# Norms by slots, idle products and a moved score in a four-layer graph kernel: layer 1's first two norms and layer 2's first on ScalarE and VectorE

## The reference

```python
def _layernorm(x, axis=-1, eps=1e-05):
    m = jnp.mean(x, axis=axis, keepdims=True)
    v = jnp.var(x, axis=axis, keepdims=True)
    return (x - m) / jnp.sqrt(v + eps)
...
        agg = jnp.einsum('nm,bmd->bnd', A_hat, features)          # layer 0
        h = jax.nn.relu(_batchnorm(x @ W1.T + b1, g1, be1))
        out = _batchnorm(h @ W2.T + b2, g2, be2)
...
        e = jnp.einsum('behd,hd->beh', jax.nn.leaky_relu(Xq[:, src] + Xq[:, dst], 0.2), a)   # layer 1
        # + log adj of the edge, softmax over the edges of one src, then
        Y = jax.ops.segment_sum(attn[..., None] * Xv[:, dst], src, num_segments=n)
        return Y @ W_out.T
...
    h = jax.nn.relu(_slconv(x, adj, S, W1))                       # layer 2: (adj*adj) @ (x @ W)
    h = jax.nn.relu(_slconv(h, adj, S, W2))
    return _slconv(h, adj, S, W3)
...
    attention = jax.nn.softmax(where(adj==0, -inf, leaky(s1+s2))) # layer 3
    h_prime = jnp.einsum('bij,bjo->bio', attention, Wh)
```

## Time and profile before

| what | value |
|---|---|
| three runs | 584.73, 585.36 (median), 586.92 us |
| the profiled execution | 586.41 us, its span 584.6 us |
| TensorE busy | 537.5 us (92% of the span) |
| VectorE busy | 423.2 us (72%) |
| ScalarE busy | 370.3 us (63%) |
| GpSimd busy | 210.5 us (36%) |
| mean granted clock of TensorE | 0.96 |

### The profile page before, as it was taken

The page is one execution under the profiler, slowest core; times in us unless marked ns, Lnnn a source line. Parts: engine busy times, 40 slices in busy tenths (PEclk is TensorE's granted clock), DMA queues, the critical chain, the costliest instruction groups (busy, mean ns, idle before and its releaser), DMA issues.

```text
span 584.6 us, 11192 instructions
## 1 busy us (share of the span) xinstructions
PE 537.5 (92%) x3482; PEld 468.7 (80%) x3482; DVE 423.2 (72%) x1454; ACT 370.3 (63%) x741; POOL 210.5 (36%) x248
## 2 busy tenths in 40 slices
PE   3999799589999879999999999999999999999872
PEld 3888433468887679898998998998998998989762
DVE  4688667778986165358879679679778776787887
ACT  3666692557755414536568768778678677675682
POOL 8830530457575240501813513514514314310103
PEclk9999799689999769999999999999999999999997
DMA  7223000221200000000000100100100100100012
...
DMA packets 28383, 15.26 MB, mean 26 GB/s; under 512 B 2320, under 2 KB 28048, under 8 KB 28352
## 3 DMA queue, kind: packets, MB, share of 16 engines
...
...
## 4 chain that ended last, share of the span: by engine, by line
PE 79%; DVE 12%; ACT 4%; issue 2%; POOL 2%; DMA 0%; DVEq 0%; POOLq 0%; ACTq 0%; SPq 0%
PE psum L238 15%; PE psum L240 14%; PE psum L239 14%; PE psum L1818 9%; PE psum L1643 6%; PE psum L1685 5%; PE psum L1760 2%; PE psum L1770 2%; PE psum L1692 2%; PE psum L1696 2%; PE psum L1706 2%; DVE ln_st L184 2%; PE psum L1864 2%; PE psum L1846 2%; POOL ln_r L203 1%
## 5 line engine op out<-in xcount | busy, mean ns | idle before, releaser
L203 POOL TENSOR_TENSOR ln_r<-ln_v,mhalf 128x8 f32<-128x8 f32 x30 | 50.0, 1666 | 238.9 <-DVE ln_v L197 238.9
L1818 PE MATMUL psum<-l2w_s,h 128*128 128x128 f32 x512 | 59.8, 275 | 0.0
L1818 PEld LDWEIGHTS psum<-l2w_s,h 128*128 128x128 f32 x512 | 59.0, 192 | 0.8
L238 PE MATMUL psum<-qt_hi,l2w_s_hi 128*128 128x512 f32 x128 | 52.7, 412 | 0.0
L240 PE MATMUL psum<-qt_hi,l2w_s_lo 128*128 128x512 f32 x128 | 50.7, 396 | 0.0
L239 PE MATMUL psum<-qt_lo,l2w_s_hi 128*128 128x512 f32 x128 | 50.6, 395 | 0.0
L232 ACT ACTIVATE keep_x<-keep_x,ln_b,ln_r (+1 forms) x108 | 44.4, 487 | 7.0 <-DVE keep_x L224 4.4
L1400 ACT ACTIVATE h<-psum 128x512 f32<-128x512 f32 x60 | 34.8, 593 | 11.7 <-PE psum L240 11.6
L184 DVE BATCH_NORM_STATS2 ln_st<-keep_x 128x6 f32<-128x128 f32 (+1 forms) x192 | 39.4, 278 | 2.9 <-ACT keep_x L1328 1.6
L238 PE MATMUL psum<-wgt_hi,h_hi 128*128 128x256 f32 x128 | 37.1, 290 | 0.9 <-DVE h_lo L888 0.9
L240 PE MATMUL psum<-wgt_hi,h_lo 128*128 128x256 f32 x128 | 35.8, 280 | 0.0
...
## 6 DMA issues: line engine op xcount, KB each, us to landing
...
```

Of the source, the lines that this page charges most:

```text
L203: pool.tensor_tensor(ln.r[:].rearrange("p s k -> p (s k)"), ln.v[:].rearrange("p s k -> p (s k)"), mhalf[:], ALU.pow).then_inc(ln.root, 1)
L238: pe.matmul(o, lhs[0], rhs[0], start=start, stop=False)
L1818: i = pe.matmul(bank(s)[:, 0, k * D:(k + 1) * D], h2[:, s, g, j * N + t * P:j * N + (t + 1) * P], l2w3_s[:, g, :], start=(g == 0), stop=(g ...
```

## The change

Six things change, with new semaphores to match.

1. TensorE gets idle products, `spin(n, bank)`: n fp32 products of `ident` with `iota_row` (256 columns) whose result nobody reads. Four stand before the transposes of `dinv` and four behind them, six behind the edge sort, three behind the products for `adj_dst`, and three ahead of the first gather.
2. The layer norms after layer 0 of slots 0 to 3 (`ln0`) and after layer 1 of slots 0 and 1 (`ln1`) are taken slot by slot (`first_stats`, `first_moments`, `first_power`). For slots 0 and 1 VectorE norms two of the four quarters and ScalarE the other two (`first_apply`, `first_scale`); slots 2 and 3 are normed by VectorE alone. ScalarE makes the high half, VectorE the low half, for slots 0 and 1 of `ln0` by graph (`x1_high_low`). GpSimd keeps the powers alone.
3. GpSimd forms `prod` only when VectorE's coefficients (`bn2_ready`) are done.
4. The order ahead of layer 1's loop is `gather(0)`, `project(0)`, `gather(1)`, `score(0)`, `project(1)` among `turn_out` 1 to 4, and the loop begins at 2. ScalarE's `bn_out` runs three steps ahead, no longer four, and slot by slot between the copies of the gathered rows.
5. At the end of layer 1 the order of gather, attend, output and score changes, `turn_attention(0)` moves ahead of `project(6)`, and the second half of step 1's attention goes to bank 2 (before: bank 7).
6. The scores of layer 1's last step are formed inside `mix_x` of layer 2's first step, and VectorE takes the scores (`take_scores(1)`) behind `pt_low`.

```diff
+        def first_stats(dve, q, ln):
+            dve.wait_ge(ln.added, q + 1)
+            for k in range(4):
+                i = dve.bn_stats(ln.st[:, q % 2, k, :], xn[:, q, k // 2, k % 2, :])
+            i.then_inc(ln.one_stats if q < 2 else ln.stats, 1)
+        def first_moments(dve, q, ln, shared):
+            s = q % 2
+            if q < 2:
+                dve.wait_ge(ln.one_stats, q + 1)
+            else:
+                dve.wait_ge(ln.stats, q - 1)
+            for k in range(4):
+                i = dve.bn_aggr(ln.ag[:, s, k, :], ln.st[:, s, k, :])
+            i.then_inc(ln.one_mean, 1)
+            dve.wait_ge(ln.one_mean, q + 1)
+            if shared:
+                dve.tensor_scalar(ln.m[:, s], ln.ag[:, s, :, 0], -1.0, None, ALU.mult)
+            dve.tensor_scalar(ln.v[:, s], ln.ag[:, s, :, 1], LN_EPS, None, ALU.add).then_inc(ln.one_var, 1)
+        def first_power(pool, q, ln, shared):
+            s = q % 2
+            pool.wait_ge(ln.one_var, q + 1)
+            pool.tensor_tensor(ln.r[:, s], ln.v[:, s], mhalf[:, 0:4], ALU.pow).then_inc(ln.one_root, 1)
+            if shared:
+                pool.wait_ge(ln.one_root, q + 1)
+                pool.tensor_tensor(ln.b[:, s], ln.m[:, s], ln.r[:, s], ALU.mult).then_inc(ln.one_rstd, 1)
+        def first_apply(dve, q, ln, ks, done, by):
+            s = q % 2
+            dve.wait_ge(ln.one_root, q + 1)
+            for k in ks:
+                y = xn[:, q, k // 2, k % 2, :]
+                i = dve.tensor_scalar(y, y, ln.ag[:, s, k, 0:1], ln.r[:, s, k:k + 1], ALU.subtract, ALU.mult)
+            i.then_inc(done, by)
+        def first_scale(act, q, ln, ks, done):
+            s = q % 2
+            act.wait_ge(ln.one_rstd, q + 1)
+            for k in ks:
+                y = xn[:, q, k // 2, k % 2, :]
+                i = act.activation(y, y, ACT.Identity, bias=ln.b[:, s, k:k + 1], scale=ln.r[:, s, k:k + 1])
...
             pool.wait_ge(adj_dst_out, 1)
+            pool.wait_ge(bn2_ready, 1)
             pool.tensor_tensor(prod[:], adj_dst[:], ssrc[:], ALU.mult).then_inc(picked, 1)
...
-            ln_power(pool, 0, ln0)
-            for s in range(2):
-                split_x1(0, s, True)
-            ln_power(pool, 1, ln0)
-            with pool.Fori(1, IT - 1) as p:
+            for q in range(4):
+                if q >= 2:
+                    pool.wait_ge(ln0_done[1], q - 1)
+                first_power(pool, q, ln0, q < 2)
+            ln_power(pool, 2, ln0)
+            with pool.Fori(2, IT - 1) as p:
...
-            ln_power(pool, 0, ln1)
-            for s in range(2):
-                split_x(0, s, True)
+            for s in range(2):
+                first_power(pool, s, ln1, True)
+            pool.wait_ge(xs_lo, 2)
...
+            sum0_slot(0, 0)
+            first_stats(dve, 0, ln0)
+            first_moments(dve, 0, ln0, True)
+            sum0_slot(0, 1)
+            first_stats(dve, 1, ln0)
+            first_apply(dve, 0, ln0, (0, 2), ln0_done[0], 1)
+            first_moments(dve, 1, ln0, True)
+            for j in range(2):
+                x1_high_low(0, j)
+            sum0_slot(1, 0)
+            first_apply(dve, 1, ln0, (0, 2), ln0_done[0], 1)
+            first_stats(dve, 2, ln0)
+            for j in range(2):
+                x1_high_low(1, j)
+            first_moments(dve, 2, ln0, False)
+            sum0_slot(1, 1)
+            first_stats(dve, 3, ln0)
+            first_apply(dve, 2, ln0, range(4), ln0_done[0], 2)
+            first_moments(dve, 3, ln0, False)
+            x1_low(2)
+            leaky_slot(0, 0)
+            first_apply(dve, 3, ln0, range(4), ln0_done[1], 2)
+            sum0_slot(2, 0)
+            x1_low(3)
+            sum0_slot(2, 1)
+            leaky_slot(0, 1)
+            variance0(2, False)
+            sum0(3)
+            apply0(2)
+            body(1, False)
+            with dve.Fori(2, IT - 3) as p:
...
+            for s in range(2):
+                leaky_slot(IT - 2, s)
+                weighted_low(0, s)
...
+            weighted_low(1, 0)
+            add(0, 0, o1_done, 1, ln1)
+            first_stats(dve, 0, ln1)
+            first_moments(dve, 0, ln1, True)
+            weighted_low(1, 1)
+            add(0, 1, o1_done, 6, ln1)
+            first_apply(dve, 0, ln1, (0, 2), ln1.done, 1)
+            first_stats(dve, 1, ln1)
+            first_moments(dve, 1, ln1, True)
+            xs_low(0)
+            leaky_slot(IT - 1, 0)
+            first_apply(dve, 1, ln1, (0, 2), ln1.done, 1)
+            xs_low(1)
+            leaky_slot(IT - 1, 1)
...
+                if early:
+                    early(1)
...
+            for p in range(2):
+                for s in range(2):
+                    bn_out_slot(p, s, p == 0)
+            bn_out_slot(2, 0, False)
+            first_scale(act, 0, ln0, (1, 3), ln0_done[1])
+            for j in range(2):
+                x1_high(0, j)
+            bn_out_slot(2, 1, False)
+            first_scale(act, 1, ln0, (1, 3), ln0_done[1])
+            for j in range(2):
+                x1_high(1, j)
+            gathered(0)
+            x1_high_both(2)
+            projected(0, 0)
+            x1_high_both(3)
+            projected(0, 1)
+            for s in range(2):
+                bn_out_slot(3, s, False)
+                gathered_slot(1, s)
+            scale0(2)
+            for s in range(2):
+                projected(1, s)
+            for s in range(2):
+                bn_out_slot(4, s, False)
+            edge_log()
+            scale0(3)
+            with act.Fori(2, IT - 3) as p:
...
+            for s in range(2):
+                gathered_slot(IT - 1, s)
+                y1_turned(0, s, 6 - 6 * s)
+                weighted_high(1, s, False)
+            first_scale(act, 0, ln1, (1, 3), ln1.one_scaled)
+            xs_high(0)
             for s in range(2):
                 projected(IT - 1, s)
...
+                        y1_turned(p + 1, s, 2 if s and first else 6 + s)
...
+            def spin(n, psum_bank):
+                for _ in range(n):
+                    pe.matmul(bank(psum_bank)[:, 0, 0:N], ident[:], iota_row[:], start=True, stop=True)
+            spin(4, 7)
...
             i.then_inc(dinv_spread, 1)
+            spin(4, 7)
...
+            spin(6, 0)
...
             i.then_inc(adj_dst_done, 1)
+            spin(3, 2)
...
             turn_out(0, True)
-            turn_out(1, False)
+            turn_out_slot(1, 0, False)
             pe.wait_ge(picked, 1)
             for t in range(T):
                 i = pe.matmul(bank(6)[:, 0, 0:E], ones[:], prod[:, t, :], start=(t == 0), stop=(t == T - 1))
             i.then_inc(a_edge_done, 1)
+            turn_out_slot(1, 1, False)
+            spin(3, 2)
+            gather(0, True)
             turn_out(2, False)
-            gather(0, True)
+            project(0)
+            gather(1, False)
             turn_out(3, False)
-            project(0)
+            score(0)
+            project(1)
+            turn_out(4, False)
...
+                    if first:
+                        score_slot(IT - 1, s)
...
+                    if first and s == 1:
+                        pe.wait_ge(y1_out, 4)
                     if ahead and not first:
+                        if behind and not two_behind:
+                            pe.wait_ge(sm, SM_STEPS + 1)
...
+            gather_slot(IT - 1, 0, False)
             pe.wait_ge(sm, SM_STEPS)
             attend1(0, 0, 6)
+            gather_slot(IT - 1, 1, False)
+            pe.wait_ge(ln0.added, Q)
+            output1(0, 0, 1)
+            attend1(0, 1, 0)
             score(IT - 2)
-            pe.wait_ge(ln0.added, Q)
-            attend1(0, 1, 0)
+            output1(0, 1, 6)
             project(IT - 1)
-            output1(0, 0, 1)
-            output1(0, 1, 6)
-            score(IT - 1)
             pe.wait_ge(ln1.added, 2)
             attend1(1, 0, 6)
-            pe.wait_ge(sm, SM_STEPS + 1)
-            attend1(1, 1, 7)
+            pe.wait_ge(z_ready, Q - 1)
+            attend1(1, 1, 2)```

TensorE at the first norms of layer 1. Before, from the transposes of `bnt` for slot 2 on (`picked` is GpSimd's `prod`, `x1_lo` a split slot):

```order
L1672 MATMUL psum<-ident,bnt 128x128 [waits ln0_added,bnt_ready]
L1672 MATMUL psum<-ident,bnt 128x128 x3
L1716 MATMUL psum<-prod,ones 128x256 [waits picked]
L1716 MATMUL psum<-prod,ones 128x256
L1672 MATMUL psum<-ident,bnt 128x128 [waits ln0_added,bnt_ready]
L1672 MATMUL psum<-ident,bnt 128x128 x3
L1672 MATMUL psum<-ident,bnt 128x128 [waits ln0_added,bnt_ready]
L1672 MATMUL psum<-ident,bnt 128x128 x3
L1685 MATMUL psum<-sel,x1s_hi 128x512 [waits x1_lo]
```

230 lines of the change are left out of this document (123 added, 107 removed).

## The result

| kernel | runs | median us | lowest to highest | ratio to before, 95% interval |
|---|---|---|---|---|
| before | 4 | 585.97 | 584.73 to 586.92 | 1 |
| changed | 4 | 568.58 | 567.21 to 569.82 | 0.9707 (0.9678 to 0.9736) |

A forecast was written before the change was run, and what follows sets the result against it. TensorE bounds nearly everywhere, save three half-clock stretches, with norm paths holding two layer starts. Terms 1.4 + 2.9 + 3.8 + 12.0 = 20.1 us off 586.41 give 566.3, or 565.3 against the median; range 561.5 to 572.

The forecast's parts named there:

- The end of layer 1: Gather 7 to layer 2's first hidden layers: 24.1 us instead of 36.1, gaining 12.0 us; bounds 7 and 13.9.
- the 13.9 us of loss before: Gather 7 to layer 2's first hidden layers: 36.1 us beyond 22.2 of full-clock work, put down to half clock and waits.
- The second pass: Layer 0's second pass: six idle products keep the clock up, 5.8 us at half clock take 2.9; gain 2.9 us.
- `prod`: Behind the coefficients: GpSimd's `prod`, held until `bn2_ready`, no longer meets VectorE's one-element instruction; gain 0.95 us.
- The start: First products at full clock through idle products, ranking about 1 us sooner; gain 1.4 us, bounds 0 and 2.3.
- The first norms: Layer 1's start up to gather(3): norms slot by slot bring gathers sooner; gain 3.8 us including 0.95 for `prod`.
- the rival with a chance of 0.20: Clock still falls at one or two thin places (`bnt` wait, first norms, layer 2's first step): 569 to 572 us; 0.20.
- the main case: Whole kernel, "as summed": all four terms come out near their forecasts, 562 to 568 us; chance 0.55.
- the case of one or two falls: Whole kernel: TensorE's clock still falls at one or two thin places, 3.4 us each; 569 to 572 us, chance 0.20.
- VectorE beside GpSimd's power: First norms: VectorE's low halves running beside GpSimd's powers lose nothing, going by the earlier trace's row.
- the 1 us that I derived from the rule: First norms: by the skill's shared-pair rule they would lose about 1 us more, four powers deep; not counted.

The follow-up runs named there:

- prod_free: Changed kernel, but GpSimd's `prod` no longer waits for VectorE's coefficients (`bn2_ready`), as before the change; 569.17 us in one run.
- scores_before: Changed kernel with layer 1's last scores, and the leaky steps and copies feeding them, ahead of layer 2's first step; 570.65 us, ratio 0.9747 to before.
- norms_together: Changed kernel with VectorE norming both slots of layer 2's first norm together, ScalarE's and TensorE's orders kept; 573.86 us, ratio 0.9791 to before.

## Why the prediction was right, and where it was off

**The end of layer 1** (12.0 forecast, 12.1 measured) was right in size, and the new state was as walked. TensorE is busy 22.35 us and idle 1.60 us of the 23.95, where the sum had 22.2 and 1.9: 1.02 of `h_hi` and 0.50 of `y1t` make the wait, and taking it away gave 1.9. Counted from gather 7, the split slots are ready after 12.5 and 16.0 us (walked: 12.9 and 15.9) and needed after 14.4 and 16.8 (14.6 and 16.9).

What was wrong is how the 13.9 us of loss before were split. I counted 10.2 us of half clock there; the trace has 17.1 (6.8 from 196.3 on, which the window of 210 to 225 does not see, and 10.2 from 210.0), and TensorE was idle only 6.0 of the 36.06 us. So 7.7 of the 12.1 us are busy time that got shorter (30.06 to 22.35), and 4.4 are waits that went. That did not touch the forecast, which adds up the work that stays.

Undoing parts lost 4.2 (the norm by slots) and 2.1 us (the scores' place), each with a fall of 3.4 us in it. The remaining part, the order of attends, outputs and projection, was not undone alone.

**The second pass** (2.9, measured 2.7) and **`prod`** (0.95, measured 0.94) were each undone alone and lost 2.6 and 0.9 us.

**The start** is the term that was mis-sized: 1.4 forecast, -1.1 measured. The step that failed was "the ranking needs GpSimd's comparisons, which end at 15.9 whatever TensorE does. So it can start about 1 us sooner". The comparisons do set it, but they were 1.44 us late, and then a fall of 3.4 us at 20.1, behind TensorE's wait of 2.36, cost 1.0 (68.8 where 15.48 + 52.3 gives 67.8). With the comparisons at 14.04 and the hop of 52.3 the pass would start 67.73 - (14.04 + 52.3) = 1.4 us sooner, an estimate: the step fails because the comparisons did not stay where they were, and the rest of the term stands. Whether the idle products delay the load stays open: the comparisons began at 14.0, 14.4 and 15.2 in the three kernels without them and at 14.6 to 15.6 in the eleven with them.

**The first norms** were forecast at 2.85 behind `bnt` and gave 2.0. The first gather came 7.1 us behind `bnt` (7.4 walked). Beyond it the clock fell at 139.5, the rival with a chance of 0.20. What that fall costs can be read without an edit: g0-g3 is 36.0 or 36.1 us in the six kernels of the table that have one fall of 3.4 us at 137 to 142 us, and 34.4 in prod_free and scores_before, whose instructions there are the same and whose clock stays up. That is 1.7 us, half of 3.4. Without the fall the term would have been 3.7, above the forecast. The rival's mechanism held beside the main case, at one place and at its price. The total is nearer than its terms: the path without the fall was 0.9 us shorter than summed, and that hid half of what the fall cost.

So 2.5 of the 3.4 us that are missing lie in the start and 0.9 here. The median, 568.58, lies between the main case (562 to 568) and the case of one or two falls (569 to 572). The profiled execution was one of the two upper ones (569.67 and 569.82 against 567.48 and 567.21).

**VectorE beside GpSimd's power.** I priced this at nothing by the earlier trace rows, and that was wrong. Here are the powers of layer 1's first two slots and of layer 2's first one, with VectorE's subtractions of two SBUF inputs that start just ahead of them:

```profile
105.29 1.02 POOL L239 TENSOR_TENSOR ln_r<-ln_v,mhalf 128x4 f32<-128x4 f32 x1 [2.67 <-DVE ln_v L233]
107.85 1.28 POOL L239 TENSOR_TENSOR ln_r<-ln_v,mhalf 128x4 f32<-128x4 f32 x1 [1.26 <-DVE ln_v L233]
191.23 1.38 POOL L239 TENSOR_TENSOR ln_r<-ln_v,mhalf 128x4 f32<-128x4 f32 x1 [4.25 <-DVE ln_v L233]
...
107.84 0.76 DVE L912 TENSOR_TENSOR x1s_lo<-keep_x,x1s_hi 128x256 fp32r<-128x256 f32 x2
191.06 0.68 DVE L971 TENSOR_TENSOR wv_lo<-wv,wv_hi 128x512 fp32r<-128x512 f32 x1
```

A power alone takes 1.01 to 1.03 us. The one that starts 0.01 us after a short subtraction takes 1.27 to 1.29 in all thirteen traces of the changed kernel and its variants. The two of layer 2's first norm start 0.17 us into a long one and take 1.38, except in norms_together, where no subtraction runs beside them and both take 1.01. So a power that starts second pays 0.27 or 0.37 us. VectorE pays nothing: the pair at 107.84 takes 0.76, as at 110.66 with no power beside it, though its second subtraction starts inside the power, and in the earlier trace rows, where the power starts first, neither side pays.

The Trainium skill's rule of the shared pair (SBUF — State Buffer, section "SBUF: two separate sides") says that whoever starts first has it for a whole instruction. That agrees with prod_free, where VectorE waits until `prod` ends, and in direction with the powers that start second. It does not agree with VectorE's subtractions that start inside a power and lose nothing; there the rows decide. In the first norms one of four powers paid, 0.27 us: the 1 us that I derived from the rule was too much, as 0 was too little.
